# A kernel of two attention layers: its order of steps, taken from other place tables

## What is computed

```python
x = L0_attn_x                       # (16, 512, 128)
xn = _layernorm(x, axis=-1)
x = x + _L0_attn_ref(xn, ...) + _L0_ffn_ref(xn, ...)

# _L0_attn_ref: 16 heads of 8 features; reshaped so that a softmax runs over the heads of one token
Q, K, V = proj(Wq, bq), proj(Wk, bk), proj(Wv, bv)

# _L0_ffn_ref: two layers like this, 8 heads of 64, window 64
h = shift_token(x)
q, k, v = split(h @ wqkv)
q, k = l2norm(q) * qs, l2norm(k) * ksc
q, k = rotary_xpos(q, k)
x = x + local_attention(q, k, v) @ wo
h = (norm(shift_token(x)) * lg + lb) @ w1 + b1
a, g = jnp.split(h, 2, axis=-1)
x = x + (a * gelu(g)) @ w2 + b2
```

## Time and profile before

| | |
|---|---|
| median of 3 runs | 1534.08 us (1533.03 to 1536.35) |
| the profiled execution | 1533.33 us |
| its span, first to last instruction | 1531.5 us |
| ACT busy | 1377.1 us (90%) |
| DVE busy | 1368.3 us (89%) |
| PE busy | 1364.1 us (89%) |
| POOL busy | 1215.8 us (79%) |
| DMA | 67.29 MB, mean 44 GB/s |

### The profile page before, as it was taken

One profiled execution on the slowest core, in us unless ns is written; L12 is line 12 of the kernel. 1 busy time (PEld: TensorE's weight loads), 2 busy tenths in 40 slices (PEclk: granted clock), 3 DMA queues, 4 the chain that ended last, 5 costly groups with the idle time before them and its releaser, 6 DMA issues.

```text
span 1531.5 us, 40141 instructions
## 1 busy us (share of the span) xinstructions
PE 1364.1 (89%) x14680; PEld 1088.5 (71%) x14680; DVE 1368.3 (89%) x2207; ACT 1377.1 (90%) x4243; POOL 1215.8 (79%) x1385
## 2 busy tenths in 40 slices
PE   2578899899999999999999999999999989987886
PEld 1356677677777777777777777777776777776665
DVE  6999899999999999999999999999999898877641
ACT  2289797999999999999999999999999999987992
POOL 4786887889898888989898888889888886875641
PEclk8689999999999999999999999999999999999998
DMA  6021112131221222121221222112212212101110
GB/s 164 11 38 34 20 36 51 24 65 35 46 51 45 41 49 53 42 47 32 52 48 38 50 49 50 45 37 41 51 41 45 50 42 46 35 17 32 41 47 15
DMA packets 177492, 67.29 MB, mean 44 GB/s; under 512 B 146917, under 2 KB 152338, under 8 KB 177298
## 3 DMA queue, kind: packets, MB, share of 16 engines
q1 hardware_dynamic: 177154, 64.67, 20.0%
q10 hardware_dynamic: 144, 0.07, 0.0%
HBM read 17.01 MB, written 8.39 MB: 17 GB/s over the span
## 4 chain that ended last, share of the span: by engine, by line
ACT 62%; PE 16%; DVE 13%; issue 7%; DMA 1%; SPq 0%; POOL 0%; POOLq 0%; ACTq 0%; DVEq 0%
ACT sb_pl L683 17%; ACT sb_pl L690 10%; ACT sb_pT L625 6%; ACT sb_sq L660 5%; PE banks L1033 3%; ACT sb_kT L625 3%; ACT sb_hn L706 3%; ACT sb_v L625 3%; ACT sb_qT L625 3%; ACT sb_oTl L625 2%; ACT sb_gate L720 2%; PE banks L921 2%; PE banks L922 2%; PE banks L923 2%; ACT L720 2%
## 5 line engine op out<-in xcount | busy, mean ns | idle before, releaser
L683 ACT ACTIVATE sb_pl<-banks,sb_nml 128x128 f32<-128x128 f32 x1024 | 371.2, 447 | 10.7 <-DVE sb_nml L860 10.3
L586 POOL TENSOR_TENSOR sb_qk<-sb_qk,sb_t 128x1024 f32<-128x1024 f32 x128 | 305.0, 2383 | 28.2 <-DVE sb_t L845 28.2
L581 POOL TENSOR_TENSOR sb_pr<-sb_qkvf 128x2048 f32<-128x2048 f32 x64 | 293.6, 4588 | 11.7 <-DVE banks L805 9.0
L683 ACT ACTIVATION_READ_ACCUMULATOR sb_pl<-banks,sb_nml 128x1 f32 x1024 | 284.3, 289 | 0.0
L599 POOL TENSOR_TENSOR sb_qk<-sb_qk,sb_rn 128x1024 f32<-128x1024 f32 x128 | 245.2, 1916 | 11.6 <-POOL sb_rn L556 0.9
L690 ACT ACTIVATE sb_pl<-sb_pl,sb_rl 128x128 f32<-128x128 f32 x768 | 251.0, 463 | 3.4 <-DVE sb_rl L865 3.4
L921 PE MATMUL banks<-sb_wqh,sb_hh 128*128 128x512 f32 x384 | 177.0, 461 | 39.6 <-DVE sb_t L845 32.7
L860 DVE TENSOR_REDUCE sb_nml<-banks 128x4 f32<-128x512 f32 x256 | 164.1, 684 | 37.1 <-PE banks L1001 35.7
L840 DVE TENSOR_TENSOR sb_qk<-banks,sb_tab 128x1024 f32<-128x1024 f32 x128 | 155.2, 1212 | 19.7 <-ACT sb_sq L660 18.6
L660 ACT ACTIVATE sb_sq<-banks 128x1024 f32<-128x1024 f32 x128 | 136.3, 1065 | 32.8 <-PE banks L923 32.7
L845 DVE TENSOR_TENSOR sb_t<-banks,sb_tab 128x512 f32<-128x512 f32 x256 | 164.0, 684 | 0.0
(11 more groups left out here) (121 smaller groups left out, 3526.8 us busy)
## 6 DMA issues: line engine op xcount, KB each, us to landing
sb_vs<-sb_v SPq DMA_DIRECT2D x224, 128.0 KB, 2.3
sb_xt<-x SPq DMA_DIRECT2D x16, 256.0 KB, 3.0
heads_scratch<-sb_ofs SPq DMA_DIRECT2D x64, 64.0 KB, 4.2
sb_orow<-heads_scratch SPq DMA_DIRECT2D x16, 256.0 KB, 3.0
sb_ob<-x SPq DMA_DIRECT2D x16, 256.0 KB, 2.9
out<-sb_ob SPq DMA_DIRECT2D x16, 256.0 KB, 2.0
sb_hh<-sb_sh SPq DMA_DIRECT2D x16, 128.0 KB, 2.4
sb_hl<-sb_sl SPq DMA_DIRECT2D x16, 128.0 KB, 2.4
```

The costliest lines, as they stand in the source:

```text
L581: nc.gpsimd.tensor_tensor(pr[:].rearrange("p (q k d) -> p q k d", q=H, k=H), q[:, :, None, :].to_broadcast([P, H, H, D]), k[:, None, :, :] ...
L586: nc.gpsimd.tensor_tensor(qk[:, k, :], qk[:, k, :], t2[:, TURN[step] % 2, :], ALU.add).then_inc(s_add.sem, 1)
L683: last = nc.scalar.activation(pl[:, k, m, :], ps[:, m * P:(m + 1) * P], ACT.Exp, bias=nml[:, k, m:m + 1], accum_out=suml[:, k, m:m + 1])
```

## The change

Only the numbers of the tables are changed: 208 slots, and the 30 places and scales of the first and last units and heads. The same steps are done, each with the same instructions; what changes is the sorted list, and with it the order in each of the five queues, the bank of each product and the step that releases it. The core of the diff:

```diff
--- before.py
+++ after.py
@@ -40,62 +40,62 @@
...
-FIRST_AT = (-1.0956341, 0.4576868, 1.7427875, 2.5433456, 3.8219324)
-LAST_AT = (-4.8382878, -2.9062629, -0.9651967, -1.1040628, 0.1136649)
-FIRST_SCALE = (1.0499025, 0.9358336, 0.9592917, 0.9938125, 1.0304354)
-LAST_SCALE = (0.9670584, 0.7425029, 0.4668260, 0.7402405, 0.6229305)
+FIRST_AT = (-1.4170251, 0.3756808, 1.3160665, 2.5476465, 3.9180029)
+LAST_AT = (-4.8394308, -3.1107710, -1.0246412, -1.3060719, -0.3138637)
+FIRST_SCALE = (1.0487257, 0.8910786, 1.0051510, 0.9589559, 1.0141119)
+LAST_SCALE = (0.9634352, 0.7966739, 0.5233979, 0.7862088, 0.7329170)
...
-HEADS_AT = (0.4634402, 0.7559115, 2.5889320, -4.5843117, -1.7930715)
-HEADS_SCALE = (0.6122646, 0.9697668, 1.0901495, 0.9335650, 0.7285575)
+HEADS_AT = (0.7262329, 1.3544475, 1.4511646, -4.8497848, -2.3781911)
+HEADS_SCALE = (0.5863118, 0.7897658, 1.2846532, 0.9610227, 1.0873477)
...
 UNIT_SLOTS = {
-    "project_qk": (161.5337, 170.4979, 185.6540, 197.6936), "square": (162.9646, 171.9673, 188.0445, 197.7300),
-    "rope": (166.4026, 178.7795, 190.3739, 207.6947), "ssq": (171.4809, 174.1664, 195.1606, 200.8458),
...
-    "v_copy": (191.7705, 210.1239, 228.8074, 232.5426), "move_v": (199.7911, 216.0315, 231.7321, 246.6051),
...
-    "k_copy": (192.5553, 202.9064, 217.2686, 226.2716), "scores": (197.7789, 206.6406, 219.6917, 228.3139),
...
-    "exp": (201.2002, 201.5570, 210.5060, 212.6741, 221.9340, 224.6950, 233.2779, 233.8987),
...
-    "out_local": (259.6125,), "x2": (264.5936,), "shift_x2": (269.3621,), "stats2": (270.9225,), "aggr2": (272.2621,),
...
-    "up": (286.8409, 287.2442, 291.9634), "gelu": (287.2379, 287.2540, 293.9063), "up_copy": (294.2196,),
...
+    "project_qk": (180.8865, 189.9008, 200.8035, 207.4905), "square": (182.8332, 191.3764, 202.6269, 215.0484),
+    "rope": (185.6095, 196.5146, 203.8132, 222.4632), "ssq": (194.5791, 196.4048, 212.7382, 218.0087),
...
+    "v_copy": (208.3649, 235.7447, 244.8661, 250.4572), "move_v": (241.6022, 245.0766, 257.6514, 259.7270),
...
+    "k_copy": (210.8460, 222.6798, 236.6207, 244.9249), "scores": (214.6428, 226.7933, 236.6746, 249.8680),
...
+    "exp": (218.0782, 219.9987, 231.6306, 232.2496, 240.8241, 243.3168, 254.0171, 255.7111),
...
+    "out_local": (280.4230,), "x2": (282.3611,), "shift_x2": (286.4764,), "stats2": (288.8477,), "aggr2": (290.4905,),
...
+    "up": (304.6119, 306.2553, 308.4325), "gelu": (306.1736, 307.3863, 309.7276), "up_copy": (310.5655,),
...
 FIRST_SLOTS = {
-    "shift_x": (132.5675,), "x1": (302.3450,), "shift_x1": (306.0756,), "x1_t": (308.9108,), "x1_split": (309.8298,),
...
+    "shift_x": (156.3497,), "x1": (319.1466,), "shift_x1": (322.3211,), "x1_t": (323.9081,), "x1_split": (326.0269,),
...
 IN_SLOTS = {
-    "load": (-16.0142,), "stats": (-8.0778,), "aggr": (-7.4563,), "rstd1": (51.0225,), "norm": (56.5504,),
-    "norm_t": (83.1148,), "x_split": (87.4672,), "x_low": (89.7965,),
+    "load": (-5.0639,), "stats": (5.0259,), "aggr": (55.4120,), "rstd1": (70.0568,), "norm": (76.1918,),
+    "norm_t": (129.3316,), "x_split": (132.1203,), "x_low": (135.2987,),
...
 HEADS_SLOTS = {
...
-    "product": (128.0713, 153.2039, 180.7110, 205.7647), "full_scores": (141.7959, 162.3482, 188.3189, 212.9234),
-    "full_max": (145.2027, 165.1950, 191.0109, 216.5427), "full_less": (147.5240, 166.9261, 194.6915, 224.0911),
...
-    "heads": (208.2411, 221.0684, 245.4143, 276.6383),
...
+    "product": (149.6120, 176.3338, 200.4536, 229.4578), "full_scores": (165.0038, 184.2047, 212.2232, 235.3917),
+    "full_max": (167.7649, 189.6126, 215.4059, 238.9628), "full_less": (168.6540, 192.2515, 218.1399, 242.0238),
...
+    "heads": (208.5262, 241.6488, 270.6775, 282.9770),
...
 OUT_SLOTS = {
-    "heads_load": (249.2093,), "attn_t": (270.1900,), "o_t": (271.3115,),
+    "heads_load": (287.7618,), "attn_t": (288.7107,), "o_t": (290.2221,),
...
 PREP_SLOTS = {
-    "weights": (103.0881, 103.9758, 112.0775, 134.5225, 148.9447), "split_w3": (80.3243,), "high_q": (120.0702,),
-    "split_q": (93.0556, 139.0609), "tables": (73.0399, 87.2460), "fold": (150.0609,), "gain": (150.6569,),
-    "high_up": (177.5070,), "split_up": (226.6600,), "biases": (164.8906,),
+    "weights": (98.3366, 111.2558, 114.1553, 117.1637, 117.5111), "split_w3": (114.1842,), "high_q": (146.0354,),
+    "split_q": (114.0363, 147.5037), "tables": (112.6202, 113.3247), "fold": (173.0347,), "gain": (189.4362,),
+    "high_up": (192.3543,), "split_up": (238.4012,), "biases": (177.8621,),
...
 LAST_SLOTS = {
-    "x_again": (269.0376,), "result": (312.1891,), "add_x": (313.5121,), "store": (318.7254,),
+    "x_again": (268.4375,), "result": (322.7550,), "add_x": (325.8623,), "store": (389.2926,),
...
```

More of the change, by code:

```diff
@@ new lines @@
+    "project_qk": (180.8865, 189.9008, 200.8035, 207.4905), "square": (182.8332, 191.3764, 202.6269, 215.0484),
+    "rope": (185.6095, 196.5146, 203.8132, 222.4632), "ssq": (194.5791, 196.4048, 212.7382, 218.0087),
+    "rope_add": (188.1454, 206.5760, 223.4222, 233.6851), "rnorm": (201.6163, 229.9386),
+    "normed": (202.6476, 209.3313, 230.9116, 236.1666), "project_v": (207.4155, 232.8308, 242.8203, 246.9345),
+    "v_copy": (208.3649, 235.7447, 244.8661, 250.4572), "move_v": (241.6022, 245.0766, 257.6514, 259.7270),
@@ new lines @@
+    "qk_t": (209.9548, 220.0953, 236.0666, 244.3496), "q_copy": (210.7943, 221.3493, 236.2510, 244.9249),
+    "k_copy": (210.8460, 222.6798, 236.6207, 244.9249), "scores": (214.6428, 226.7933, 236.6746, 249.8680),
+    "row_max": (217.6715, 227.0768, 238.5868, 252.3728),
+    "exp": (218.0782, 219.9987, 231.6306, 232.2496, 240.8241, 243.3168, 254.0171, 255.7111),
+    "row_recip": (222.7313, 223.5714, 232.5504, 235.3187, 243.1449, 254.8964, 258.8819, 259.7251),
+    "scale": (228.2235, 232.2694, 232.9685, 238.4063, 251.2133, 259.5532, 261.1805, 262.7764),
@@ new lines @@
+    "probs_t": (236.2443, 236.5841, 237.3733, 247.6974, 262.4904, 262.7625, 265.5813, 266.5942),
+    "p_copy": (236.7764, 237.2279, 239.9596, 249.3942, 263.7704, 264.9891, 266.4087, 266.6868),
+    "values": (243.1696, 251.7666, 270.0334, 272.2945), "o_copy": (245.9943, 253.6017, 273.7925, 274.5773),
+    "out_local": (280.4230,), "x2": (282.3611,), "shift_x2": (286.4764,), "stats2": (288.8477,), "aggr2": (290.4905,),
+    "rstd2": (291.1243,), "norm2": (297.2897,), "norm2_t": (300.0493,), "high2": (300.8491,), "low2": (302.1931,),
@@ L72 @@
+    "up": (304.6119, 306.2553, 308.4325), "gelu": (306.1736, 307.3863, 309.7276), "up_copy": (310.5655,),
+    "hid": (308.3777, 308.4169), "pool_hid": (313.7593,), "down": (317.5384,),
 }
 FIRST_SLOTS = {
-    "shift_x": (132.5675,), "x1": (302.3450,), "shift_x1": (306.0756,), "x1_t": (308.9108,), "x1_split": (309.8298,),
-    "x1_low": (310.8519,),
+    "shift_x": (156.3497,), "x1": (319.1466,), "shift_x1": (322.3211,), "x1_t": (323.9081,), "x1_split": (326.0269,),
+    "x1_low": (327.0368,),
@@ L83 @@
-    "product": (128.0713, 153.2039, 180.7110, 205.7647), "full_scores": (141.7959, 162.3482, 188.3189, 212.9234),
-    "full_max": (145.2027, 165.1950, 191.0109, 216.5427), "full_less": (147.5240, 166.9261, 194.6915, 224.0911),
-    "full_exp": (148.3797, 169.3692, 198.1087, 225.9567), "full_values": (152.3746, 173.7146, 202.0788, 231.8030),
-    "full_out": (155.8941, 183.2570, 206.6652, 234.4620), "full_norm": (161.3726, 186.4811, 211.9778, 239.1022),
-    "heads": (208.2411, 221.0684, 245.4143, 276.6383),
+    "qkv_full": (140.6256, 144.6622, 151.7724, 162.0712), "qkv_bias": (143.1849, 147.0736, 153.8033, 165.2998),
@@ new lines @@
+    "product": (149.6120, 176.3338, 200.4536, 229.4578), "full_scores": (165.0038, 184.2047, 212.2232, 235.3917),
+    "full_max": (167.7649, 189.6126, 215.4059, 238.9628), "full_less": (168.6540, 192.2515, 218.1399, 242.0238),
+    "full_exp": (170.2900, 196.2990, 221.2679, 246.0143), "full_values": (175.3323, 198.7211, 224.9344, 249.0944),
+    "full_out": (178.0246, 205.0059, 230.1271, 255.4147), "full_norm": (183.9576, 210.0330, 233.9907, 264.7515),
+    "heads": (208.5262, 241.6488, 270.6775, 282.9770),
```

12 lines of the change are left out of this document (removed).

## The result

The changed kernel takes 1524.87 us (median of 4 runs, 1523.78 to 1525.94), the kernel before, beside it, 1535.09 us (4 runs, 1533.03 to 1536.35). The ratio is 0.9935 with a 95% interval of 0.9918 to 0.9952: 10.0 us less, between 7.4 and 12.6. The forecast was 1527. So the total came out near the forecast. That was luck: none of its three terms was right, and their errors cancelled. The rest of this document shows how.

A forecast was written before the change was run, and what follows sets the result against it. The prediction took ACT (ScalarE) to set the pace from 283 to 1236 us, its work unchanged, so only waits could move. From 1533.3 us, -7 + 0 + 0 gave 1526.3, as a median about 1527; range 1513 to 1543.

The forecast's parts named there:

- Term 1: Start: first unit's steps come forward, heads go back; the lead is passed on, -7 us (ends +2 and -12).
- The first step: Start, DVE's big weight split ahead of the small one: first projection at 21.2 to 23.4 us, lead taken 2 us.
- rival B: ACT and DVE of 130 to 283 us absorb the lead, or POOL is late: 1534 us, no change; chance 0.20.
- Term 2: Middle, eleven periods of 86.6 us: possible gains and new waits taken as 0 (ends -12 and +16).
- Rival A: Middle tightens too: some 12 of ACT's 16.8 us idle time go, 1515 us; chance 0.15.
- C: Middle, scores behind the shifted transpose: ACT waits 1.5 us a period, +16 with the lead kept, 1543 us; chance 0.13.
- Term 3: End of the kernel, four parts: sum 0 (ends -5 and +8).
- (a): End: DVE's head steps of the last sequence go back by 15.5 us of work behind the last unit's first rope.
- (d): Last unit: postponed head steps, in pieces of 2.28 us, come ahead of row maxima; about +1.3 us for single collisions.
- rival D: End crowded: postponed head steps push five of the last unit's maxima by 2.28 us each, +12, about 1538; chance 0.10.
- (b): End: squares and copies fill ACT's 6.43 us wait for unit (13, 1)'s normalization; together -4 us.
- (c): Last unit: PE does the down projection of (14, 1) ahead of the last out projection, +2.7 us.

The follow-up runs named there:

- e7: Kernel after with the heads' load put 20 places earlier, ahead of the shift of the residual as in the old order: 1524.46 us, ratio 0.9945 to the kernel before.
- e1: New order up to the 1134th step (383 us), old order from there on: 1534.21 us, ratio 0.9999 to the kernel before.
- e4: New order only up to the 571st step (221 us), old order behind it: 1532.32 us, ratio 0.9984 to the kernel before.
- e2: Old order with the new one only in the middle, from 383 to 1224 us: 1530.31 us, ratio 0.9970 to the kernel before.
- e8: Kernel after with ten transposes of the shifted first layer back behind the second scores: 1531.17 us, ratio 0.9987 to the kernel before.
- e3: Old order up to 1224 us, new order behind it (the end alone): 1533.37 us, ratio 0.9988 to the kernel before.
- e5: Old order up to 383 us, new order all the way behind it (middle and end): 1524.12 us, ratio 0.9943 to the kernel before.
- e11: Kernel after with the last sequence's head steps back at their old places: 1535.86 us, ratio 1.0016 to the kernel before.
- e10: Kernel after with the last out projection ahead of the down projection of unit (14, 1) again: 1522.75 us, ratio 0.9923 to the kernel before.
- e12: e4's start, new order from 383 us, e10's edit, and e7's load for the last two sequences: 1516.51 us, ratio 0.9888 to the kernel before.

## Why the prediction was right in sum and wrong in its terms

**What sets the pace: right.** ACT's work did not change, and every gain is idle time of ACT, as the first part said.

**Term 1, the start (-7; measured 0).** The first step held in its result. DVE and POOL at the start, kernel after:

```profile
16.57 1.76 DVE L756 TENSOR_TENSOR sb_wql<-sb_pl,sb_wqh 128x1536 fp32r<-128x1536 f32 x1
16.65 1.74 POOL L575 TENSOR_TENSOR sb_nmr<-sb_nmr,sb_rs 128x4 f32<-128x4 f32 x1
...
18.35 5.10 POOL L565 TENSOR_TENSOR sb_tab<-sb_tab,sb_gate 128x1024 f32<-128x1024 f32 x2
...
18.64 2.58 DVE L756 TENSOR_TENSOR sb_w3l<-sb_orow,sb_w3h 128x384 fp32r<-128x384 f32 x1
21.36 0.66 PE L921 MATMUL banks<-sb_w3h,sb_sh 128*128 128x384 f32 x1 [11.31 <-DVE sb_w3l L756]
```

The big subtraction takes 1.76 us with no product beside it, not 5.93, and is over at 18.3 us, before the 20.3 to 22.4 that I gave. The small one, which I priced under 1 us with nothing of POOL beside it, takes 2.58 us beside the table products, as before. The two errors about cancel: the first projection starts at 21.36 (21.2 to 23.4), the first rope ends at 28.3 (29.0 to 31.3). The first residual came at 115.7 us, ahead of my 117 to 121. What failed is the sentence behind it: "both orders have the same steps to do up to 283 us, so the lead is passed on unless later waits eat it". Later waits did eat it. The lead of 10 us at that residual is only 4.1 at 221 us, where equal work is done (2.9 by the means), and the new order then wastes it itself. The sign that I had named for it failed plainly: the first square of sequence 3 came at 288.16 us, not near 277, and in the kernel before at 283.56. ACT in 15 us stretches, before (245 to 275) and after (241 to 271):

```profile
245.00:260.00 15.00, 14.32 (x151) 12.52 (x150) 13.91 (x18) 10.75 (x22) 12.40 (x16) 1.00 0.22 57
260.00:275.00 15.00, 10.89 (x113) 8.57 (x112) 15.00 (x28) 10.58 (x34) 14.13 (x13) 0.85 0.15 25
```

```profile
241.00:256.00 15.00, 14.34 (x153) 12.71 (x151) 11.30 (x15) 10.20 (x19) 7.52 (x3) 1.00 0.02 4
256.00:271.00 15.00, 9.99 (x76) 7.82 (x75) 13.44 (x28) 5.04 (x10) 13.23 (x25) 0.89 0.40 81
```

ACT stands 14.8 of 30 us instead of 8.7. I read the idle 21.6 us of the 153 from 130 us on as something the new order might reduce; it grew to 33.0. Which step's place does it is not settled: e7 excludes the heads' load, e1 and e4 put the place between the 571st and the 1134th step. This is rival B, by half of its own mechanism (absorbed between 130 and 283 us), for this term alone.

**Term 2, the middle (0; measured -4.6, e2).** Rival A named the right wait and had the size wrong. The square's wait fell by 0.77 us a period, 0.27 came new at the exponentials, and the period went from 86.62 to 86.19 us, neither below A's 85.9 nor above C's 87.3. My going down the queue gave the new wait 0 to 1.5 us; it is at the low end. What failed is the 0: I let a gain of unknown size and a loss of unknown size cancel. What I did not see is that the two are one question, where PE's transpose stands against ACT's copy of it (e8). The heads' load was hidden in the middle, as taken, and not at 263.65 and 1496.45 us, where PE waits 3.8 and 5.1 us for it; removing that changed nothing that can be measured (e7).

**Term 3, the end (0; measured -1.8 alone in e3, and -4.1 as the difference of e5 and e2).** (a) with (d) is the step with the wrong sign: the postponed heads were priced at +1.3 us (rival D: +12) for the collisions at their new place, and at nothing for what they leave behind. Undone, they cost 12.5 us (e11). (b) The wait of 6.43 us went to nothing instead of to about 2.4. (c) was right as far as it went. The last out projection of the kernel after:

```profile
1487.62 3.74 PE L1033 MATMUL banks<-sb_wo_local,sb_oTl 128*128 128x128 f32 x32
```

It starts 3.61 us behind the last values (1484.01 us), where it was 0.87 and is 0.78 in e10: 2.7 us, as forecast (the sign that I had named, 4.5 us behind the last values, was set too late). But in the traces the last unit gives back 5.2 to 6.0 us. Of the 5.5 of the kernel after, 0.9 is gone before the last values, and 1.8 are lost behind the out projection, most of them in the last matmuls, kernel after and then e10:

```profile
1512.64 0.77 PE L1063 MATMUL banks<-sb_wo_full,sb_oT 128*128 128x128 f32 x2 [2.34 <-POOL sb_hid L606]
1513.20 1.49 PE L1065 MATMUL banks<-sb_wd,sb_hid 128*128 128x128 f32 x6
```

```profile
1513.11 0.46 PE L1067 MATMUL banks<-sb_wo_full,sb_oT 128*128 128x128 f32 x2 [2.31 <-POOL sb_hid L610]
1513.40 0.83 PE L1069 MATMUL banks<-sb_wd,sb_hid 128*128 128x128 f32 x6
```

The same six matmuls take 1.49 us at half the clock and 0.83 at the full one (the granted clock is 0.70 on average from 1512.6 to 1518 us in the kernel after, and 1.00 from 1513 to 1518 us in e10). In the kernel after PE had stood still for 5.1 us and then 3.2 us in this unit, and its granted clock was 0.50 from 1496.4 to 1509 us; e10 puts the down projection into the first of these gaps. That this is why its last matmuls ran at the full clock is my reading of the rows; no run tests it alone.

So the errors of the terms were +7, -4.6 and -4.1 us (or -1.8), and they cancelled by luck. The sum of the measured terms is -8.7 us with e5, inside the 7.4 to 12.6 that were measured, and -6.4 with e2 and e3 alone, which is outside but has an uncertainty of its own of some 2.5 us. The range, 1513 to 1543 us, says little: it was taken from rivals A (which stands at 1515 in the prediction's own list) and C, whose 12 and 16 us a middle that moved by 4.6 never came near, and it is 30 us wide.

## What to carry to other kernels

Judge a reordering at points where both orders have done the same set of steps on every engine, not at a landmark: a unit that is preferred comes early and proves nothing. A postponed step has two prices, the collisions where it goes and the room where it was; on the engine beside the bound the second can be the larger, here 12.5 us against the 1.3 that I had reckoned for the first. And a copy that is moved takes the DMA that waits for it along, with everything behind that DMA in its queue: here one such move, once in each of 18 units, cost 34 us in all.

## What the runs showed of the hardware

- The exclusion of DVE and POOL works both ways. In the earlier trace rows DVE's subtraction waited for POOL's product. Here POOL's product of four columns (L575) takes 1.74 us beside the subtraction and ends with it (18.39 against 18.33 us); in the kernel before the same instruction took 0.20 us. ACT's second normalization and the table products are 2.3 us later, 1.5 of it for this. The Trainium skill ("SBUF — State Buffer", section "SBUF: two separate sides") has this as an exclusive lock of a port pair that whoever starts first keeps for the whole instruction, on VectorE's side for instructions with two inputs in SBUF, as this subtraction has; the trace agrees, with 1.74 against 0.20 us.
- TensorE's granted clock differs between executions of nearly the same order: from 1350 to 1475 us it was 0.96 to 1.00, and the stretch 1224 to 1485 us then gained 7.8 to 11.0 us. Those with 0.99 or 1.00 in its second half and the new start or middle ahead of it gained 10.8 to 11.0 (the kernel after, e7, e12), those with 0.96 or 0.97 gained 7.8 to 9.2 (e5, e8, e10). What comes first, the lower clock or the waits, the runs don't tell.
